# Layer 0's differences computed on VectorE out of PSUM, the softmax bias on ScalarE, and one table for the places of the work

## The reference

```python
xn = _layernorm(x)
q, k, v = einsum(xn, wq), einsum(xn, wk), einsum(xn, wv)   # 8 heads of 128
s = rope(q) @ rope(k).T / 128 - 1e30 * mask                # causal
o = softmax(s) @ v ; attn = einsum(o, wo)
h = relu(s0 * concat([xn, -xn]) @ K0) * 2                  # K0, K1, K2 hold only +1 and -1
h = relu(s1 * h @ K1) * 2                                  # 1024 x 1024
ffn = s2 * h @ K2
out = x + attn + ffn
```

## Time and profile before

| | |
|---|---|
| median of 3 runs | 2038.27 us (2030.26 to 2038.82) |
| the profiled execution's own time | 2039.47 us |
| its span, first to last instruction | 2037.8 us |
| busy, share of the span | PE 87%, VectorE 83%, GpSimd 64%, ScalarE 62% |
| mean granted TensorE clock | 0.971 of full speed |
| chain that ended last, by engine | VectorE 50%, PE 25%, ScalarE 15%, GpSimd 6% |

### The profile page before, as it was taken

The page is one execution under the profiler, slowest core; times in us unless marked ns, Lnnn a source line. Parts: engine busy times, 40 slices in busy tenths (PEclk is TensorE's granted clock), DMA queues, the critical chain, the costliest instruction groups (busy, mean ns, idle before and its releaser), DMA issues.

```text
span 2037.8 us, 34064 instructions
## 1 busy us (share of the span) xinstructions
PE 1781.7 (87%) x12720; PEld 1210.4 (59%) x12720; DVE 1691.2 (83%) x3335; ACT 1254.7 (62%) x2587; POOL 1298.1 (64%) x1313
## 2 busy tenths in 40 slices
PE   6878979889898888988989889898988879989888
PEld 3446646656565565665656566565665646656567
DVE  7988978888788897888988788888888878889786
ACT  6666656556656565566666656565665656657553
POOL 5786666666666656666675675756656666666662
PEclk9999999999999999999999999999999999999999
DMA  4233423323333342343323333242331424325233
GB/s 150 42 56 59 92 49 79 58 51 78 59 68 58 68 73 48 68 74 68 57 47 74 67 68 63 47 88 48 74 67 42 84 50 81 58 60 81 48 58 73
DMA packets 454837, 134.07 MB, mean 66 GB/s; under 512 B 434704, under 2 KB 453648, under 8 KB 454672
## 3 DMA queue, kind: packets, MB, share of 16 engines
q1 hardware_dynamic: 454672, 131.90, 34.1%
HBM read 14.94 MB, written 8.39 MB: 11 GB/s over the span
## 4 chain that ended last, share of the span: by engine, by line
DVE 50%; PE 25%; ACT 15%; POOL 6%; issue 3%; DMA 1%; SPq 0%; DVEq 0%; POOLq 0%
PE bank L441 24%; DVE ph L653 17%; ACT p L630 9%; DVE p L616 5%; DVE hb L799 5%; DVE ta L570 5%; DVE qk L586 4%; POOL ph L647 2%; DVE o L496 2%; DVE xT L279 2%; ACT hb L794 2%; DVE h L493 2%; DVE v L496 2%; POOL tb L574 2%; DMA pt<-ph 1%
## 5 line engine op out<-in xcount | busy, mean ns | idle before, releaser
L647 POOL TENSOR_SCALAR ph<-p,ri 128x512 f16<-128x512 f32 (+3 forms) x512 | 385.0, 752 | 487.6 <-DVE rk L637 451.3
L653 DVE SCALAR_TENSOR_TENSOR ph<-p,rk,ph 128x512 f16<-128x512 f32 (+3 forms) x512 | 511.7, 1019 | 20.5 <-POOL ph L647 18.4
L576 POOL TENSOR_TENSOR ta<-ta,tb 128x512 f32<-128x512 f32 x256 | 355.9, 1390 | 86.3 <-DVE ta L570 70.5
L630 ACT ACTIVATE p<-p,nm,sc 128x512 f32<-128x512 f32 (+3 forms) x512 | 327.5, 641 | 126.8 <-DVE nm L624 126.2
L582 ACT ACTIVATE qk<-ta 128x512 f16<-128x512 f32 x256 | 160.7, 628 | 388.4 <-POOL ta L576 388.0
L441 PE MATMUL bank<-hb,wa 128*128 128x256 f16 x3360 | 391.2, 274 | 2.1 <-DVE o L496 2.1
L441 PEld LDWEIGHTS bank<-hb,wa 128*128 128x128 fp8e5 x3360 | 329.4, 99 | 53.5 <-DVE o L496 2.4
L574 POOL TENSOR_TENSOR tb<-tb,sin 128x512 f32<-128x512 f32 x256 | 330.9, 1293 | 40.6 <-ACT tb L564 28.5
L441 PE MATMUL bank<-qk 128*128 128x512 f16 (+3 forms) x1536 | 249.3, 314 | 75.7 <-DVE ri L635 46.1
L441 PE MATMUL bank<-pt,v 128*128 128x256 f16 x2250 | 232.6, 259 | 58.4 <-DVE ta L570 38.2
L799 DVE TENSOR_TENSOR hb<-rt,hb 128x768 f16<-128x768 f32 x120 | 137.5, 1146 | 172.4 <-ACT hb L794 172.2
(11 more groups left out here) (109 smaller groups left out, 2302.6 us busy)
## 6 DMA issues: line engine op xcount, KB each, us to landing
out<-xnat SPq DMA_DIRECT2D x32, 256.0 KB, 2.4
xnat<-in_x SPq DMA_DIRECT2D x15, 512.0 KB, 4.1
pt<-ph SPq DMA_TRANSPOSE x250, 4.3
o<-in_k SPq DMA_DIRECT2D x1, 1024.0 KB, 8.5
v<-in_wq SPq DMA_DIRECT2D x1, 1024.0 KB, 10.5
v<-in_wk SPq DMA_DIRECT2D x1, 1024.0 KB, 12.2
ph<-in_wv SPq DMA_DIRECT2D x1, 1024.0 KB, 13.6
o<-in_wo SPq DMA_DIRECT2D x1, 1024.0 KB, 10.7
```

What stands on the lines that cost most here:

```text
L576: done["rot", n] = pool.put(lambda e: e.tensor_tensor(ta, ta, tb, ALU.add))
L630: done["exp", g, i] = act.put(lambda e: e.activation(v, v, ACT.Exp, bias=NM[:, g % 4, i:i + 1], scale=SC[:, 0:1], accum_out=SM[:, g % 4, i ...
L647: done["P_hi", g, i] = pool.put(lambda e: e.tensor_scalar(part(r, i, HI), v, RI[:, g % 4, i:i + 1], 4096.0, ALU.mult, ALU.mult))
L653: done["P_lo", g, i] = dve.put(lambda e: e.scalar_tensor_tensor(part(r, i, LO), v, RK[:, g % 4, i:i + 1], part(r, i, HI), ALU.mult, ALU.su ...
```

## The change

- In `layer0_pair` ScalarE copies only the first of the two banks into `rt`. VectorE makes the four differences (`difference`, 128x256 each) with the ReLU applied to the bank as it reads it and the other operand out of `rt`. ScalarE makes the high parts of the second bank's two blocks straight from PSUM (128x512) and that of the third block from `rt` (128x256); VectorE makes the low parts from the two banks (128x512 and 128x256). GpSimd has no part in it any more. The two banks are held until the last difference and the low parts have been made.
- The bias `nm` is made by ScalarE (`bias`), in the queue ahead of the exponentials.
- `PLACES` names for each job of a batch the turn and an order; order 0 or 1 is before the scores, 2 or 3 between scores and values, 4 or 5 behind the values. In a steady batch three things stand elsewhere than before: `strassen` part 2 of the first column group goes behind the scores, `layer2` of the first half and the first layer 0 pair go behind the values, and the second `layer2` job changes places with the second layer 0 pair. `proj` has entries of its own and stays where it was.
- `DELAY` has new numbers for nearly every hand-over, and `SETUP` places the making of `wa` and the splitting of the weights at the start.
- Waits that named one of four results now name all four.

Cut to its core:

```diff
-V_SECOND = {0: (3, 2), 1: (3, 3), 2: (4, 2), 3: (2, 2)}
...
+PLACES = {
...
+    "seg": ((2, 0), (2, 4), (3, 2), (3, 5), (4, 0), (4, 4), (5, 2), (5, 4)),
...
-DELAY = dict(hi=0, lo=10, swap=2, straight=8, crossed=8, qhi=22, qhi_w=11, qlo=32, bias=0, exp=10, exp_i=0,
-             differ=2, keep_hi=3, keep_lo=9, t_hi=21, t_lo=27, add=3, inv=22, high=24, high_i=5, low=38, low_i=3, turned=42, x_hi=40, x_lo=50, x_turned=61)
+DELAY = dict(hi=0, lo=10.4, swap=2.8, straight=8.4, crossed=5.7, qhi=24.7, qhi_w=11, qlo=32.3, bias=10.4, exp=11.7,
+             exp_i=0.2, differ=3.2, keep_hi=0, keep_lo=4.2, t_hi=14.1, t_lo=21, add=6, inv=22.9, high=25, high_i=1.6,
+             low=37.7, low_i=7.2, turned=54.5, x_hi=41.2, x_lo=51.3, x_turned=61.5)
...
             def bias():
-                dve.wait(need(("max", g, 1)))
-                done["bias", g] = dve.put(lambda e: e.tensor_scalar(NM[:, g % 4, :], MX[:, g % 4, :], SC[:, 1:2], None,
-                                                                    ALU.mult))
+                act.wait(need(("max", g, 1)), done["scale"])
+                done["bias", g] = act.put(lambda e: e.activation(NM[:, g % 4, :], MX[:, g % 4, :], ACT.Copy,
+                                                                 scale=SC[:, 1:2]))
...
-                t1 = pool.put(lambda e: e.tensor_tensor(RT[:, 4], RT[:, 3], RT[:, 2], ALU.subtract))
-                pool.put(lambda e: e.tensor_tensor(RT[:, 5], RT[:, 1], RT[:, 3], ALU.subtract))
-                pool.wait(t1)
-                t2 = pool.put(lambda e: e.tensor_tensor(RT[:, 6], RT[:, 1], RT[:, 4], ALU.subtract))
-                pool.wait(t2)
-                done["T", b, i] = pool.put(lambda e: e.tensor_tensor(RT[:, 7], RT[:, 0], RT[:, 6], ALU.subtract))
...
+            def keep():
+                act.wait(done[top.key])
                 if i:
-                    pool.wait(need(("h0t", b, i - 1)))
...
+                    act.wait(need(("T", b, i - 1, 3)), need(("h0r_hi", b, i - 1, 0)))
+                done["r", b, i] = act.put(lambda e: e.activation(
+                    RT[:, 0:2].rearrange("p a b -> p (a b)"), top.ps[:, :], ACT.Relu))
...
+            def lo_of(f, first, last, half):
+                def run():
+                    dve.wait(need(("h0r_hi", b, i, half)))
+                    done["h0r", b, i, half] = dve.put(lambda e: e.scalar_tensor_tensor(
+                        HB[:, first:last, LO, i, :], f.ps[:, 0:256 * (last - first)].rearrange("p (a n) -> p a n", n=256),
+                        0.0, HB[:, first:last, HI, i, :], ALU.max, ALU.subtract))
...
+            def difference(n, f, col, out, other):
+                def run():
+                    dve.wait(done[f.key], need(("r", b, i)))
+                    if n != 1:
+                        dve.wait(need(("h0r_hi", b, i, 1)))
...
+                    done["T", b, i, n] = dve.put(lambda e: e.scalar_tensor_tensor(
+                        RT[:, out], f.ps[:, col:col + 256], 0.0, RT[:, other], ALU.max, ALU.subtract))
```

More of the change, by code:

```diff
@@ L610, in maxes @@
                     if g >= 2:
-                        dve.wait(need(("P_lo", g - 2, 0)))
+                        dve.wait(*[need(("P_lo", g - 2, i)) for i in range(4)])
                     else:
@@ L633, in inverse @@
             def inverse():
-                dve.wait(need(("exp", g, 0)))
+                dve.wait(*[need(("exp", g, i)) for i in range(4)])
                 done["inv", g] = dve.put(lambda e: e.reciprocal(RI[:, g % 4, :], SM[:, g % 4, :]))
@@ L658, in turned @@
             def turned():
-                sp.wait(need(("P_lo", g, 0)), done["pad"], done["W2"])
+                sp.wait(*[need(("P_lo", g, i)) for i in range(4)], done["pad"], done["W2"])
                 if home in held_by:
@@ L765, in layer0_pair @@
                         f.mm((0, 512), W0[:, c, n * 128:n * 128 + 128], XT[:, b % 2, s, :, c, :])
[L766 to L772, removed]
-                        RT[:, 2 - 2 * half:4 - 2 * half].rearrange("p a b -> p (a b)"), f.ps[:, :], ACT.Relu))
@@ new lines, in hi_of @@
+            def hi_of(f, first, last, half):
+                def run():
+                    act.wait(done[f.key] if half else need(("r", b, i)), done[read])
+                    src = f.ps[:, :].rearrange("p (a n) -> p a n", n=256) if half else RT[:, 0:1]
+                    done["h0r_hi", b, i, half] = act.put(lambda e: e.activation(
+                        HB[:, first:last, HI, i, :], src, ACT.Relu))
+                return run
+            def lo_of(f, first, last, half):
[4 more added lines that the diff above has]
+                        0.0, HB[:, first:last, HI, i, :], ALU.max, ALU.subtract))
+                return run
@@ new lines, in t_hi, with t_lo @@
+            def t_hi():
+                act.wait(need(("T", b, i, 4)), need(("T", b, i, 3)), done[read])
+                done["h0t_hi", b, i] = act.put(lambda e: e.activation(HB[:, 3:7, HI, i, :], RT[:, 4:8], ACT.Copy))
+            def t_lo():
+                dve.wait(need(("h0t_hi", b, i)))
+                done["h0t", b, i] = dve.put(lambda e: e.tensor_tensor(
+                    HB[:, 3:7, LO, i, :], RT[:, 4:8], HB[:, 3:7, HI, i, :], ALU.subtract))
+            at(0, keep)
+            at(DELAY["differ"], difference(1, top, 256, 4, 0))
@@ L998, in block_kernel @@
+            if b < NB - 1:
+                place(b, "proj", *[lambda b=b, k=k: proj(b, k) for k in range(2)])
         for slot, heads in LAST:
-            add_filler(G + slot, 4, lambda heads=heads: proj_last(heads))
+            fillers.setdefault(G + slot, []).append((4, lambda heads=heads: proj_last(heads)))
         def normal(b):
@@ L1022, in block_kernel @@
         convert_k1(act, 5, 8)
-        combine(3)
-        combine(4)
         largest(0, "q")
```

156 lines of the change are left out of this document (67 added, 89 removed), and 9 rows, old and new, of the table PLACES.

## The result

The median is 1799.74 us (1799.23 to 1800.66, 4 runs) against 2037.35 us of the kernel before (2030.26 to 2038.82, 4 runs). The ratio is 0.884, 95% interval 0.8819 to 0.8862: 238 us less, where 92 were forecast, and outside the range.

A forecast was written before the change was run, and what follows sets the result against it. Neither PE nor VectorE is full; each head's work passes between them. VectorE's -84 - 20 - 15 = -119 us, 75% carried, is -89; with the start -92, from 2039.5: 1947, set at 1946 us; range 1880 to 2022.

The forecast's parts named there:

- the bias's wait in ScalarE's queue: `bias` waits for the last maximum at ScalarE's queue head; costed at nothing, 0.6 us a head without scores' lead.
- the moved fillers: Same matmuls on PE in other places; costed at nothing, else PE waits at a fill behind layer 0's two banks.
- the delays: Order of the probabilities' low parts on VectorE, priced by GpSimd's holds; -15 us, near none, as two effects oppose.
- layer 0: Per layer 0 pair on VectorE: differences added, bias and high-part wait gone; -1.40 us a pair, -84 us in all.
- start -3: PE idle in the first two windows; spreading `wa` may give some of it; -3 us, 0 to -12.
- Rival 2: Saving comes back in front of the inverse, differences standing on the path; some 25 us left, 2014 us; chance 0.12.
- Rival 5: VectorE stands at the first difference until ScalarE has copied one bank and made the other's high part; 2077 us; chance 0.06.
- Rival 4: In the Strassen stretch low parts come later and each meets a GpSimd sine product; slower, 2053 us; chance 0.07.
- The carry of 75%: The chain lies on PE for 25%, so 75% of VectorE's saving reaches the end: -119 us becomes -89.
- the cap: In the layer 0 stretch PE's idle time limits the saving: 15 x 6.94 = 104 us.
- Rival 1: PE becomes the bound: layer 0 stretch loses all 104 us, Strassen stretch and start 50 more; 1885 us; chance 0.12.
- The signs: `hb` wait under 30 us, difference 0.41, GpSimd 190 less busy, layer 0 PE idle under 3, low parts at most 1.0.

The follow-up runs named there:

- b_l0: The kernel before with the new layer 0 and its five delays alone, all else old; 1972.2 us.
- a_bias: The changed kernel with the bias back on VectorE, at its new delay of 10.4; 1942.0 us.
- a_bias_dve0: The changed kernel with the bias on VectorE right behind the maxima (delay 0), the exponentials at their new delay; 1842.3 us.
- a_low_old: The changed kernel with only the delays of the high and low parts of the probabilities put back; 1869.8 us.
- b_bias: The kernel before with the bias on ScalarE alone, its delay 0 as before; 2081.3 us.
- a_start_old: The changed kernel with the old setup and the old places of layer 1 and the first V jobs of batch 0; 1793.2 us.
- b_delay_rest: The kernel before with the new delays except those of the bias, the exponentials and layer 0; 1958.6 us.

## Why the prediction was wrong, point by point

The steps that failed are three terms of the sum: the bias's wait in ScalarE's queue and the moved fillers, both put at nothing, and the delays, put at -15 us on VectorE. At the end of the span the forecast is, like for like, layer 0 -50, bias -29, delays -11, fillers 0, start -3. The runs have layer 0 -62, bias and its place -67, the rest of the delays -80, fillers -68, start 0: -277, of which 238 came.

- **Layer 0: right in kind, and its size hit by luck.** The -84 us on VectorE hold 18 of the bias in 60 heads; without them they are -66 (1.64 + 0.13 - 2.87 = -1.10 a pair), and 75% of that is 50, where both runs say 62. The prices were right: the differences took 0.419 us each for 0.41, the 128x256 low part 0.415 for 0.41, VectorE's wait for `hb` went to 4.6 us (16.9 in b_l0). GpSimd is busy 177 us less for 187. Rival 2, a saving that comes back in front of the inverse, came in small with layer 0 alone (60.9 us of waits there in b_l0, for 37.9) and not in the change (24.1). Rival 5, a stall at the differences, did not come: VectorE is idle 10.8 us in front of them.
- **The bias: the step that failed first.** I saw that a wait is put into ScalarE's queue and asked only what is held behind it, costing that at nothing. For all 128 heads I had -38 us on VectorE, 29 of them carried. At the old delay the move costs 47 us and at the new one it gives 67, a swing of 114 us by a number of the table that I had listed and not priced. The other value that I named for what is held behind, 0.6 us a head or 77 us, is near what the old place costs (47 us lost where 29 were forecast as gained), but it was not in the sum. What the table does is to have ScalarE do its copies first and reach the bias when the maxima are ready.
- **The delays, -15 us: the second step that failed.** I priced the order of the low parts by GpSimd's holds alone, and took it for the whole of the delays, which give 80 us. The low parts did become cheaper against the kernel before, by 74 us of VectorE's time and not 15, but not by the new order: with the old one they are cheaper still, and the kernel 70 us slower. My 0.94 us for them came from two windows; over the span it was 1.02. Rival 4 rested on the same wrong price.
- **The moved fillers, nothing: the third.** "The same matmuls" is true and tells nothing, since what PE waits for depends on what was done just before. It is 68 us alone, 105 in company.
- **The start, -3 us:** the setup gives 0, the new places of batch 0 cost about 6.
- **The carry of 75% and the cap.** Layer 0 carried 62 of the 66 us that I had for it, and the bias and the fillers gave more than VectorE's time that they save, so the share of the chain was no measure of it. The idle time of the Strassen stretch, 5.78 of 62 us, I took for a remainder; PE is now idle 0.88 of 54 there. And I counted PE's busy time as fixed, while it fell by 54 us; the clock accounts for up to 43 of them.
- Rival 1, PE as the bound at 1885 us, was the nearest in kind. It took 154 us out of PE's idle time, where 185 went, and none out of its busy time, where 54 went.
- **The signs.** The wait for `hb`, the price of a difference, GpSimd's relief, PE idle under 3 us in the layer 0 stretch (0.31) and low parts under 1.0 us all came about as written, though the time was far off. They looked at layer 0 and the low parts; none looked at ScalarE's wait for the maxima or at PE's for `layer2`.
- One reading of the range was wrong: cheap low parts, at -74 us, give 1872, which lies outside it too.

## What to carry to other kernels

In a kernel of in-order queues, price every row of a table of hand-overs by what stands directly behind it and when its input comes, not by the engine time of the rows that carry a name in the title. A short instruction that waits for another engine belongs about where its input comes, not before (+139 us here) and not much later (+12), and in front of it the work that is ready; work that is wanted last should let pass what is wanted first, even if it then takes longer itself. And where the matmul engine pauses for some microseconds at a time, a removed pause can give more than its own length through the clock, as it did behind nine of 14 pauses of 3.2 us here.

## What the runs showed of the hardware

- The bias of 128x4 on ScalarE takes 0.297 us, about as long as on VectorE in the kernel before (0.304 us) and more than the one-column copy (0.203 us) from which I had bounded it. On VectorE it depends on the place: 0.267 us in b_l0, 0.394 in a_bias, 0.713 in a_bias_dve0. Why was not tried.
- A difference of 128x256 out of PSUM with one SBUF input means 0.419 us in the change and 0.421 in b_l0, while the low parts with two SBUF inputs meant 0.81 us in a_low_old, 0.87 in the change and 1.02 in the kernel before: in these runs the price of the low parts depends on their place, that of the differences does not.
- In the slowest kernel of the study (b_bias) the mean granted clock was 0.957, in the fastest (a_start_old) 0.995. At 2079.5 and 1789.7 us of span that is 89 and 9 us lost to the clock, up to 80 of the 290 us between them. The clock does not order the kernels by itself: b_delay_rest has 0.967 at 1957.0 us of span, the kernel before 0.971 at 2037.8.
